# Attention products of both pairs in the second half of a turn, and a copy placed ahead of a layer norm, in a two-layer graph network on one core

## What is computed

```python
# layer 0: 8 heads of 32
nx = ln(x) * g1 + b1;  q, k, v = nx @ wq + bq, nx @ wk + bk, nx @ wv + bv
s = q k^T / sqrt(32) + where(adj > 0, 0.1 * adj * adj, -inf)
x1 = x + (softmax(s) @ v) @ wo + bo
n2 = ln(x1) * g2 + b2
x2 = x1 + gelu(n2 @ w1 + b1) @ w2 + b2            # hidden size 1024
# layer 1: one head of 256
s = (x2 Wq)(x2 Wk)^T / sqrt(256), masked by adj == 0
out = ln(x2 + (softmax(s) @ (x2 Wv)) @ Wo + bo) * gamma + beta
```

## Time and profile before

| | before |
|---|---|
| median of 3 runs | 933.11 us (933.03 to 935.66) |
| the profiled execution's own time | 931.25 us |
| its span from first to last instruction | 929.5 us |
| granted TensorE clock, mean | 0.993 of full |
| PE, PEld busy | 904.0, 806.2 us |
| DVE, ACT, POOL busy | 690.7, 641.6, 389.4 us |
| DMA | 26.29 MB, 28 GB/s |

### The profile page before, as it was taken

How to read it: one execution, slowest core, us unless ns; L and a number is a source line. 1 busy time by engine, 2 the same in 40 slices (tenths; PEclk the granted TensorE clock), 3 DMA queues, 4 the chain that set the end, 5 groups by cost and what they waited for, 6 DMA issues and landing times.

```text
span 929.5 us, 22591 instructions
## 1 busy us (share of the span) xinstructions
PE 904.0 (97%) x7623; PEld 806.2 (87%) x7623; DVE 690.7 (74%) x2578; ACT 641.6 (69%) x1888; POOL 389.4 (42%) x258
## 2 busy tenths in 40 slices
PE   8889999999999999999999999999999999999996
PEld 8677798988889898888989889898888989888796
DVE  6676877869587795958779586787958778685846
ACT  5685957668486775858667595866849576684842
POOL 3424153542625355262634516254361635434222
PEclk9999999999999999999999999999999999999998
DMA  7101000010101001010100101010010100000001
GB/s 261 35 1 35 2 24 24 25 35 0 55 1 34 23 23 34 0 34 23 34 23 23 34 0 34 23 34 23 8 48 0 34 23 23 17 2 24 1 24 35
DMA packets 29743, 26.29 MB, mean 28 GB/s; under 512 B 1142, under 2 KB 29452, under 8 KB 29708
## 3 DMA queue, kind: packets, MB, share of 16 engines
q1 hardware_dynamic: 29692, 25.83, 8.9%
q10 hardware_dynamic: 16, 0.00, 0.0%
HBM read 17.44 MB, written 8.39 MB: 28 GB/s over the span
## 4 chain that ended last, share of the span: by engine, by line
PE 42%; issue 21%; POOL 14%; DVE 14%; ACT 7%; POOLq 1%; DVEq 0%; ACTq 0%
PE bank L339 10%; PE bank L341 9%; PE bank L340 9%; DVE nx L1138 4%; POOL x L1612 4%; DVE hT_lo L1064 3%; PE bank L483 3%; POOL y L1617 3%; PE bank L588 3%; PE bank L613 3%; ACT bank L874 3%; PE bank L475 2%; POOL adj_s L1561 2%; ACT bank L849 2%; POOL bias L1570 2%
## 5 line engine op out<-in xcount | busy, mean ns | idle before, releaser
L849 ACT ACTIVATE bank<-p_s,neg_max 128x128 f32<-128x128 f32 x512 | 182.1, 356 | 23.9 <-DVE neg_max L1167 23.6
L1537 POOL TENSOR_TENSOR rstd<-ve,minus_half 128x4 f32<-128x4 f32 (+1 forms) x49 | 52.9, 1079 | 302.1 <-DVE ve L1131 302.1
L339 PE MATMUL bank<-w_hi,hT_hi 128*128 128x256 f32 x512 | 147.6, 288 | 0.0
L341 PE MATMUL bank<-w_hi,hT_lo 128*128 128x256 f32 x512 | 144.2, 282 | 0.0
L340 PE MATMUL bank<-w_lo,hT_hi 128*128 128x256 f32 x512 | 144.1, 281 | 0.0
L1167 DVE CUSTOM_DVE_ANT_0 p_s<-bank,bias 128x128 f32<-128x128 f32 x512 | 112.5, 284 | 8.3 <-PE bank L475 8.2
L339 PE MATMUL bank<-n2T_hi,w_hi 128*128 128x512 f32 (+1 forms) x272 | 109.8, 404 | 3.3 <-DVE qk_lo L1065 3.3
L874 ACT ACTIVATE bank<-bank,vec_cols 128x512 f32<-128x512 f32 (+1 forms) x136 | 86.5, 636 | 30.6 <-PE bank L341 30.6
L341 PE MATMUL bank<-n2T_hi,w_lo 128*128 128x512 f32 (+1 forms) x272 | 103.9, 382 | 0.0
L340 PE MATMUL bank<-n2T_lo,w_hi 128*128 128x512 f32 (+1 forms) x272 | 103.6, 381 | 0.0
L339 PEld LDWEIGHTS bank<-w_hi,hT_hi 128*128 128x128 f32 x512 | 96.4, 188 | 2.6 <-DVE hT_lo L1064 0.8
(11 more groups left out here) (215 smaller groups left out, 2463.1 us busy)
## 6 DMA issues: line engine op xcount, KB each, us to landing
xs<-in_x SPq DMA_DIRECT2D x15, 512.0 KB, 3.8
out<-y SPq DMA_DIRECT2D x14, 512.0 KB, 3.0
adj_i<-in_adj SPq DMA_DIRECT2D x15, 256.0 KB, 2.8
out<-y SPq DMA_DIRECT2D x3, 256.0 KB, 2.2
x2T_f<-in_L_gnn_w SPq DMA_DIRECT2D x1, 512.0 KB, 6.8
tT<-in_L_gnn_w SPq DMA_DIRECT2D x1, 512.0 KB, 8.0
y<-in_L_gnn_w SPq DMA_DIRECT2D x1, 512.0 KB, 6.4
vo<-in_L_gnn_w SPq DMA_DIRECT2D x1, 512.0 KB, 7.2
```

The lines of the kernel that those rows point to most:

```text
L339: mm(out, a_hi, b_hi, start=first, stop=False)
L341: return mm(out, a_lo, b_hi, start=False, stop=last)
L849: last = run(bank[r][:, NODES * place:NODES * place + NODES], p_s[:, r, place, :], ACT.Exp, scale=-1.0, bias=neg_max[:, r, place:place + 1 ...
L1537: P.tensor_tensor(t["rstd"][:, 0:k], t["ve"][:, 0:k], minus_half[:, 0:k], ALU.pow).then_inc(ln_pool[n], 1)
```

## The change

The values' products and output projections of pair 0 move out of the MLP's up tiles to stand beside those of pair 1; for this, pair 1 gets its own places (`pT_of`, `avT_of`, banks 2 and 3). On ACT the two copies of pair 0's transposes stand behind gelu's fourth tile and no longer behind the second, on DVE they alternate with `h_low`. DVE copies t ahead of norm 2's rows. In turn (16, 15, 14) `scores1(gb)` goes ahead of `n2_transpose`. New waits: `scores(ga, 1)` for the copies of pair 0's transposes (in place of `residual1`), the first `attend` for ACT's first copy of pair 1's transposes, and `biased(gp, 0, 0)` for the values' products.

```diff
+        pT_of = (pT, p_s)
+        avT_of = ([a[:, :, :] for a in avT], [h[:, 0, :].rearrange("p (h n) -> p h n", h=4) for h in hT])
-        av_bank, wo_bank = 0, 1
+        av_bank, wo_bank = (0, 2), (1, 3)
@@ PE, scores(g, q)
-                pe.wait_ge(dve_x1, pair0(g) + q)
+                if q == 0:
+                    pe.wait_ge(dve_x1, pair0(g))
+                else:
+                    pe.wait_ge(act_pT, 2 * pair0(g) + 2)
+                    pe.wait_ge(dve_pT, 2 * pair0(g) + 2)
@@ PE, turn
                     mlp_up(gb, 4, A)
-                if A:
-                    attend(ga, 0)
                 if B:
                     mlp_up(gb, 5, A)
                 if B:
                     mlp_up(gb, 6, A)
-                if A:
-                    out_project(ga, 0)
...
                 if A2:
+                    pe.wait_ge(act_pT, 2 * pair0(ga) + 3)
+                    attend(ga, 0)
                     attend(ga, 1)
...
                 if A2:
+                    out_project(ga, 0)
                     out_project(ga, 1)
...
+                if is_last(gp):
+                    scores1(gb, P)
                     n2_transpose(ga, P, B)
-                if B:
-                    scores1(gb, P)
-                if P:
                     scores(gp, 0)
+                else:
+                    if A:
+                        n2_transpose(ga, P, B)
+                    if B:
+                        scores1(gb, P)
+                    if P:
+                        scores(gp, 0)
@@ ACT, turn
                     gelu(gb, 0)
                     gelu(gb, 1)
+                if B:
+                    gelu(gb, 2)
+                    gelu(gb, 3)
                 if A:
                     pT_copy(ga, 0, 0)
                     pT_copy(ga, 0, 2)
                 if B:
-                    for j in range(2, 5):
-                        gelu(gb, j)
-                if A:
-                    attn_high(ga, 0)
-                if B:
-                    for j in range(5, HT):
+                    for j in range(4, HT):
                         gelu(gb, j)
...
                     pT_copy(ga, 1, 0)
                     pT_copy(ga, 1, 2)
+                if A2:
+                    attn_high(ga, 0)
+                    attn_high(ga, 1)
                 if P:
                     v_copy(gp, 0)
-                if A2:
-                    attn_high(ga, 1)
@@ DVE, turn: attn_low, residual1 and sums2 of pair 0 leave the first half
                 if A2:
                     pT_copy(ga, 1, 1)
                     pT_copy(ga, 1, 3)
+                    attn_low(ga, 0)
                     attn_low(ga, 1)
                 if B:
                     x2T_low(gb)
                 if A2:
+                    residual1(ga, 0, B)
+                    sums2(ga, 0)
                     residual1(ga, 1, B)
                 if A2:
                     sums2(ga, 1)
                     moments(2, ga)
+                if B:
+                    t_copy(gb)
                 if A and B:
                     norm2(ga)
-                if B:
-                    t_copy(gb)
```

More of the change, by code:

```diff
@@ L493, in attend @@
                     for r in range(HPT):
-                        last = mm(bank[av_bank][HD * r:HD * r + HD, nodes(place)], v[:, b, HPT * t + r, :],
-                                  pT[:, r, place, :], start=True, stop=True, tile_position=(0, HD * r))
+                        last = mm(bank[av_bank[q]][HD * r:HD * r + HD, nodes(place)], v[:, b, HPT * t + r, :],
+                                  pT_of[q][:, r, place, :], start=True, stop=True, tile_position=(0, HD * r))
                 last.then_inc(pe_av, 1)
@@ L503, in out_project @@
                     for t in range(KT):
-                        last = mm3(bank[wo_bank][:, row(b)], both(avT, ALL, 2 * b + t), both(wo_p, ALL, t),
+                        last = mm3(bank[wo_bank[q]][:, row(b)], both(avT_of[q], ALL, 2 * b + t), both(wo_p, ALL, t),
                                    t == 0, t == KT - 1)
@@ L854, in pT_copy @@
                 act.wait_ge(pe_pT, 4 * (pair0(g) + q) + r + 1)
-                run(pT[:, r, :, :], bank[r][:, :].rearrange("p (h n) -> p h n", h=4), ACT.Identity).then_inc(act_pT, 1)
+                run(pT_of[q][:, r, :, :], bank[r][:, :].rearrange("p (h n) -> p h n", h=4), ACT.Identity).then_inc(act_pT, 1)
             def high_wo():
@@ L862, in attn_high @@
                 act.wait_ge(pe_av, pair0(g) + q + 1)
-                act.wait_ge(pe_wo, pair0(g) + q)
-                identity(avT[0][:, :, :], bank[av_bank][:, :].rearrange("p (h n) -> p h n", h=4)).then_inc(act_attn, 1)
+                act.wait_ge(pe_wo, pair0(g))
+                identity(avT_of[q][0], bank[av_bank[q]][:, :].rearrange("p (h n) -> p h n", h=4)).then_inc(act_attn, 1)
             def n2T_copy(g):
@@ L1164, in biased @@
                     dve.wait_ge(pool_bias, g + 1)
+                    dve.wait_ge(pe_av, pair0(g))
                 dve.sem_inc(stand_dve, 1)
@@ L1181, in pT_copy @@
                 dve.wait_ge(pe_pT, 4 * (pair0(g) + q) + r + 1)
-                V.tensor_copy(pT[:, r, :, :], bank[r][:, :].rearrange("p (h n) -> p h n", h=4)).then_inc(dve_pT, 1)
+                V.tensor_copy(pT_of[q][:, r, :, :], bank[r][:, :].rearrange("p (h n) -> p h n", h=4)).then_inc(dve_pT, 1)
             def low_wo():
@@ L1189, in attn_low @@
                 dve.wait_ge(act_attn, pair0(g) + q + 1)
-                low(avT[1][:, :, :], bank[av_bank][:, :].rearrange("p (h n) -> p h n", h=4),
-                    avT[0][:, :, :]).then_inc(dve_attn, 1)
+                low(avT_of[q][1], bank[av_bank[q]][:, :].rearrange("p (h n) -> p h n", h=4),
+                    avT_of[q][0]).then_inc(dve_attn, 1)
             def residual1(g, q, B):
@@ L1198, in residual1 @@
                         dve.wait_ge(pool_x1b, g)
-                V.tensor_tensor(x1[:, of_pair(q), :], bank[wo_bank][:, :].rearrange("p (b d) -> p b d", b=2),
+                V.tensor_tensor(x1[:, of_pair(q), :], bank[wo_bank[q]][:, :].rearrange("p (b d) -> p b d", b=2),
                                 x_bo[:, of_pair(q), :], ALU.add).then_inc(dve_x1, 1)
@@ L1325, in turn @@
                     h_low(gb, 0)
-                if A:
-                    pT_copy(ga, 0, 1)
-                    pT_copy(ga, 0, 3)
                 if C:
@@ L1332, in turn @@
                     h_low(gb, 1)
+                if A:
+                    pT_copy(ga, 0, 1)
                 if B:
                     h_low(gb, 2)
-                if P:
-                    sums1(gp)
                 if A:
-                    attn_low(ga, 0)
+                    pT_copy(ga, 0, 3)
                 if B:
@@ L1341, in turn @@
                 if P:
+                    sums1(gp)
                     moments(1, gp)
@@ L1344, in turn @@
                     norm3(gc)
-                if A:
-                    residual1(ga, 0, B)
                 if B:
@@ L1353, in turn @@
                     norm1(gp)
[L1354 to L1357, removed]
                 if A2:
```

## The result

The changed kernel takes **919.27 us** (median of 4 runs, 916.77 to 919.84); the kernel before took 933.07 beside it (4 runs, 931.52 to 935.66). The ratio is 0.9844, 95% interval 0.9815 to 0.9873. Run once more, the same kernel gave 919.15 us and a ratio of 0.9867 (0.9847 to 0.9886). The forecast was 922.3 us: right in direction and in its list of gains, but 10.8 us of gain where the medians give 13.8, about a quarter too small.

The account below looks back on a forecast made before the run. PE's own order was taken to set the turn; 0.64 us in 12 steady turns (7.7) plus 1.7, 0.5 and 0.9 from outer turns gave 10.8 us, so 933.11 becomes 922.3 us, with an 80% range of 919 to 928.5.

Parts of the forecast that it names:

- the q wait: PE's wait in the q projection for DVE's copy of t, behind norm 2's rows: moving the copy ahead gains 0.40 a turn.
- Up tiles to scores: PE's first half, up tile 4 to the scores: four up tiles in one piece take 5.76 us, before 8.44.
- The rivals on those two margins: `mlp_down` awaits `h_low(gb, 4)`: 926 us, 11 in 100; `n2_transpose` awaits norm 2's rows: 929 us, 8 in 100.
- those two margins: Time to spare in a steady turn: 0.15 us for `h_low(gb, 4)` at `mlp_down`, 0.6 for norm 2's rows at `n2_transpose`.
- turn (2, 1, 0): Turn ahead of turn (3, 2, 1): gain of 1.7 us, about 1.5 from the late t copy, plus 0.2.
- The end: The rest of the run behind turn (16, 15, 14): forecast gain 0.
- the 0.9 of turn (16, 15, 14): Turn behind the steady ones: half of PE's 1.89 us idle gained, with `scores1` ahead of `n2_transpose` filling norm 2's time.
- the side-by-side term: Pair 0's values' products and output projection beside pair 1's on PE: 0.24 a steady turn, bounds 0.10 and 0.35.
- My own bound of 0.35: Upper bound of the 0.24 a turn from pair 0's moved work, if nothing is left to pay ahead of the scores.
- turn (3, 2, 1): Turn just ahead of the steady ones: gain of 0.5 us, as ACT is late and part is lost at `mlp_down`.
- the 0.2: Part of the 1.7 us forecast for turn (2, 1, 0), added to about 1.5 from the t copy.

## Why the prediction was too small

**Right.** What sets the turn is PE's own order, and the q wait is worth 0.39 of the 0.40 forecast. Up tiles to scores take 5.76, `mlp_down` follows with 0.2 to spare and `n2_transpose` with 0.6. The rivals on those two margins didn't come true, but neither was idle talk: the first takes 0.89 a turn as soon as ACT's copies stand two tiles earlier, and the second shows in turn (2, 1, 0) with the output projections apart. The end is as forecast. So is the 0.9 of turn (16, 15, 14), but that was luck: I had taken half of the wait for the copy and reckoned with the swap, and it is the copy's move with 1.04, less 0.2 for the rest. One sentence of the working is wrong without harm: the t projection was to end "0.65 us earlier", where its own sum gives 0.24 (468.53 to 468.29); in the trace it ends 0.39 earlier in the turn.

**Wrong: the size of the side-by-side term.** The step was: "The products take 1.01 us [...], an output projection 1.43: 2.44 us that leave the first half and come back in the second". The 2.68 that leave the first half were right (8.44 to 5.76). The 2.44 that come back were not: the pair 0 product comes back as 0.90, its output projection as 1.42, and the rest of the second half is 0.02 quicker, so the term is 0.38 (0.24 + 0.11 + some 0.03) and not 0.24. My own bound of 0.35 was too low as well, because I looked for holds only between matmuls of the neighbours, whereas the time of a block, taken from its start to the next start, holds the cost of leaving it. The experiment with x2's transposes between puts 0.33 on one separation; the remaining 0.05 of the 0.38 went at the output projection among the up tiles (1.47 there in the mean of the twelve turns, 1.42 now). In twelve turns this term misses by 12 x 0.14 = 1.7 us.

**Wrong: turn (3, 2, 1).** The step was: "0.5, as ACT is late there and part is lost at `mlp_down`". Measured are 1.52. In that turn, before, PE waited for `attn_low` ahead of pair 0's output projection, after the last matmul of up tile 6. Before, DVE and PE there:

```profile
109.56 0.69 DVE L1064 TENSOR_TENSOR avT_lo<-bank,avT_hi 128x512 fp32r<-128x512 f32 x1 [0.85 <-ACT avT_hi L794]
```
```profile
109.38 0.39 PE L341 MATMUL bank<-n2T_hi,w_lo 128*128 128x512 f32 x1
110.31 0.39 PE L339 MATMUL bank<-wo_hi,avT_hi 128*128 128x256 f32 x1 [0.54 <-DVE avT_lo L1064]
```

A matmul every 0.23 would have given 109.61, so this cost 0.70. With the output projection in the second half the wait is gone, and next to nothing is lost at `mlp_down` (1.15 from the scores' start to it, for 1.10), because tiles 2 and 3 leave ACT 0.96 earlier, which I had counted for the steady turns and forgot for this one. With ACT's copies put back this turn takes 55.42, and so loses 0.98 of the 1.52. After, at the same place, PE and then DVE:

```profile
110.14 1.17 PE L484 MATMUL bank<-kT,qT 32*128 32x128 f32 x32
111.29 0.38 PE L344 MATMUL bank<-w_hi,hT_hi 128*128 128x256 f32 x1
```
```profile
109.90 0.73 DVE L1151 TENSOR_SCALAR y<-y,mv,rstd 128x256 f32<-128x256 f32 x2
110.55 1.88 DVE L1077 TENSOR_TENSOR hT_lo<-bank,hT_hi 128x512 fp32r<-128x512 f32 x3
```

So 0.78 as in every turn and 0.70 of the wait: 1.48 of the 1.52. The two parts alone agree: with the t copy alone this turn gains 0.38, with the side-by-side order alone 1.03, together 1.41.

**Wrong: turn (2, 1, 0)**, 2.29 for 1.7. The step was: "with the 0.2 I take 1.7". By blocks, q goes from 4.25 to 2.80, 1.45 for the 1.5 forecast; it is the 0.2 that was mis-sized, and 0.84 are left for it. Of these, 0.61 lie at up tiles 4 to 7, which take 3.63 us in three pieces before and 3.02 in one after (half as wide as in a steady turn, where this gives 0.20), and 0.13 at the two products. What the holds of 0.1 to 0.27 around the pieces are in that turn, separation or short waits, is open. The two parts alone give 1.23 (48.90) and 0.79 (49.34), 0.27 less than both together: q gains its 1.45 with the t copy alone too, but that profile has a wait that the profile of the kernel before doesn't show, ahead of pair 0's output projection:

```profile
62.15 0.39 PE L339 MATMUL bank<-wo_hi,avT_hi 128*128 128x256 f32 x1 [0.21 <-DVE avT_lo L1064]
```

**The sum.** The turns gave 14.0 where I had 10.8: 1.6 more from the steady turns (9.32 - 7.7), 1.0 from turn (3, 2, 1), 0.6 from turn (2, 1, 0). From 933.11 this is 919.1, beside a measured median of 919.27; with starts that scatter by 2 us (last section), that they meet so closely is chance.

## What to carry to other kernels

Price a block of PE work that uses another tiling from a place where it stands alone and from one where it stands beside its like: a start-to-start time contains the cost of leaving it, and here that made 0.11 of 1.01 us look like product. When work leaves an engine's tight half, go through each turn that isn't steady for waits that the moved work was causing, since a wait that leaves with it is a gain of its own (0.70 us here). And a reordering on the bounding engine needs its suppliers reordered with it: here, without the move on ACT, the whole gain of 0.78 a turn was lost (the move on ACT by itself was not run).

## What the runs showed of the chip beyond that

Runs of one kernel fall into groups about 2 us apart: the ten of the kernel with ACT's copies back lie at 929.62 to 930.23 and at 931.80 to 932.11. The profiles point to the granted clock in the first 30 us. Of the change, window by window, first profile and then the second:

```profile
20.00:25.00 5.00, 5.00 (x31) 5.00 (x31) 4.42 (x14) 3.44 (x18) 2.91 (x3) 0.64 0.28 95
25.00:30.00 5.00, 4.17 (x24) 3.96 (x23) 2.14 (x4) 2.56 (x5) 4.66 (x4) 0.68 0.00 0
```
```profile
20.00:25.00 5.00, 5.00 (x33) 4.80 (x33) 3.69 (x11) 2.38 (x13) 4.12 (x4) 0.70 0.39 118
25.00:30.00 5.00, 3.23 (x48) 2.62 (x47) 3.87 (x6) 3.94 (x8) 3.68 (x3) 0.96 0.00 0
```

The clock granted is the third number from the end. The first profile was at the lower of TensorE's two levels (1.2 of 2.4 GHz) for much of both windows, the second mainly in the first; 24 matmuls against 48 were done in the second window, and the stretch ahead of the turns took 48.85 and 46.10 us. The profile of the kernel with the t copy alone has a lower stretch somewhere else, at 10 to 15 us (0.69), and a start of 48.04. Across the ten profiles the start is 46.1 to 46.3 or 47.9 to 48.9, in kernels of either order, and the kernel before was profiled with 46.29. The granted clock of 25 to 30 us goes with it: 0.93 to 1.00 in the four profiles with the short start, 0.68 to 0.84 in the six with the long one. So a gain of 1 or 2 us is better read from the turns than from the median of three runs. What decides where the clock falls in a given run, with the same instructions, the runs do not show.
